# An audio-tower kernel: TensorE's attention product ahead of the transposes of the next pair's probabilities

## The reference

```python
h = tok(x)                         # importance of each row by a 2-layer GELU MLP, then pooling to 375 rows
h = h + attn(layernorm(h))         # 8 heads of 64, causal, with distance bias, q/k/v by a 3-tap filter
h = h + ffn(layernorm(h))          # 16 experts, each takes its top tokens; and one shared MLP
```

```python
q = split_heads(proj(xp, wq1, wqd)) * scale
k = split_heads(proj(xp, wk1, wkd))
v = split_heads(proj(xp, wv1, wvd))
sim = einsum("bhid,bhjd->bhij", q, k) + bias * slopes      # then masked to j <= i
out = einsum("bhij,bhjd->bhid", softmax(sim), v)
return out.transpose(0, 2, 1, 3).reshape(b, n, 512) @ wout.T
```

## Time and profile before

| | |
|---|---|
| median of 3 runs | 1357.37 us (1357.0 to 1360.63) |
| the profiled execution | 1359.58 us, its span 1357.8 us |
| TensorE busy (matmul) | 1199.7 us, 88% of the span, 7812 matmuls |
| TensorE weight loads | 1002.9 us, 74% |
| VectorE / ScalarE / GpSimd busy | 892.8 us (66%) / 731.9 us (54%) / 407.8 us (30%) |
| DMA | 42.94 MB, mean 32 GB/s |

### The profile page before, as it was taken

How to read it: one execution, slowest core, us unless ns; L and a number is a source line. 1 busy time by engine, 2 the same in 40 slices (tenths; PEclk the granted TensorE clock), 3 DMA queues, 4 the chain that set the end, 5 groups by cost and what they waited for, 6 DMA issues and landing times. The chain is left out here.

```text
span 1357.8 us, 23184 instructions
## 1 busy us (share of the span) xinstructions
PE 1199.7 (88%) x7812; PEld 1002.9 (74%) x7812; DVE 892.8 (66%) x2614; ACT 731.9 (54%) x1845; POOL 407.8 (30%) x379
## 2 busy tenths in 40 slices
PE   7999999999958999999999999999984998767663
PEld 6999999999946777777777777777763777555452
DVE  5656566665558888888888888988864878122210
ACT  2444534434346778887777888877872441322210
POOL 5000001300023323234443333441111000688885
PEclk9999999999958999999999999999997998987877
DMA  5000000000000000000000000000002000454542
GB/s 140 28 13 24 12 24 13 24 12 13 1 24 12 1 25 25 25 25 19 13 21 25 25 25 25 19 14 9 14 14 61 24 23 4 110 89 82 93 76 36
DMA packets 91800, 42.94 MB, mean 32 GB/s; under 512 B 31066, under 2 KB 88007, under 8 KB 91687
## 3 DMA queue, kind: packets, MB, share of 16 engines
q1 hardware_dynamic: 67207, 33.49, 9.1%
q0 software_dynamic: 23808, 6.69, 3.8%
q10 hardware_dynamic: 672, 1.31, 0.3%
HBM read 28.22 MB, written 9.65 MB: 28 GB/s over the span
## 5 line engine op out<-in xcount | busy, mean ns | idle before, releaser
L485 PE MATMUL bank<-h1hl,W2hl 128*128 128x376 f32 x1536 | 278.9, 337 | 2.6 <-DVE h1hl L638 2.6
L485 PEld LDWEIGHTS bank<-h1hl,W2hl 128*128 128x128 f32 x1536 | 265.2, 190 | 7.2 <-issue 4.3
L1051 ACT ACTIVATE P<-P,nmax 125x375 f32<-125x375 f32 (+2 forms) x384 | 188.9, 501 | 3.6 <-DVE nmax L1182 3.6
L585 ACT ACTIVATE h<-bank,b2c 128x375 f32<-128x375 f32 x128 | 73.6, 575 | 211.2 <-PE bank L485 211.2
L226 POOL TENSOR_SCALAR cellmax<-grid,csb 125x375 f32<-125x375 f32 x96 | 124.2, 1304 | 207.3 <-DVE csb L219 140.8
L1182 DVE CUSTOM_DVE_ANT_0 P<-bank,nbias 125x375 f32<-125x375 f32 (+2 forms) x384 | 138.9, 410 | 6.0 <-PE bank L888 5.8
L1061 ACT COPY PT<-bank 128x500 f32<-128x500 f32 (+1 forms) x256 | 127.3, 550 | 5.3 <-PE bank L907 3.1
L888 PE MATMUL bank<-QK 64*125 64x375 f32 (+2 forms) x768 | 117.7, 411 | 2.4 <-DVE nmax L1182 2.4
L901 PE MATMUL bank<-ident,P 125*128 125x125 f32 x768 | 111.1, 271 | 5.1 <-ACT P L1051 4.5
L1069 ACT ACTIVATE tap<-bank,qkd 128x375 f32<-128x375 f32 x128 | 68.6, 570 | 82.6 <-PE bank L941 82.5
L1649 ACT ACTIVATE hE<-bank,EB 128x375 f32<-128x375 f32 x64 | 36.7, 574 | 134.3 <-PE bank L1598 131.6
(11 more groups left out here) (209 smaller groups left out, 2304.1 us busy)
## 6 DMA issues: line engine op xcount, KB each, us to landing
X<-in_x_dram SPq DMA_DIRECT2D x31, 375.0 KB
EW<-in_L_ffn_w_dram SPq DMA_DIRECT2D x32, 256.0 KB
token_table<-row SPq DMA_DIRECT2D x16, 210.9 KB
tTall<-tT SPq DMA_DIRECT2D x16, 187.5 KB, 2.5
out_dram<-oS SPq DMA_DIRECT2D x16, 187.5 KB
tTall<-in_L_tok_W_dram ACTq DMA_DIRECT2D x1, 1024.0 KB, 8.8
EB<-in_L_ffn_b_dram SPq DMA_DIRECT2D x16, 62.5 KB
tok<-token_table,ids POOLq DMA_INDIRECT x48
```

What stands on the lines that cost most here:

```text
L485: last = nc.tensor.matmul(bank[4 + m % 2][:, :NE], W2hl[:, a, k, m * 128:(m + 1) * 128], h1hl[:, p, b, k], start=(k == 0 and n == 0), stop ...
L1051: nc.scalar.activation(P[:, 2 * r + q, SEG[i]:SEG[i] + w], P[:, 2 * r + q, SEG[i]:SEG[i] + w], ACT.Exp, bias=nmax[:, 2 * r + q, i:i + 1], ...
```

## The change

In TensorE's body, the call of `attend` is moved ahead of the call of `transpose_probs`. It is made in even half-steps only, so the odd ones are as they were.

```diff
--- before.py
+++ after.py
@@ -990,12 +990,12 @@
                                 transpose_v(n, e)
                             if valid(m):
                                 project_v(m, d, m % 2)
+                        m, d = pair_before(b, c, 2)
+                        if part == 0 and valid(m):
+                            attend(m, d, u if c >= 2 else v_)
                         m, d = pair_before(b, c, 1)
                         if valid(m):
                             transpose_probs(m, d, part)
-                        m, d = pair_before(b, c, 2)
-                        if part == 0 and valid(m):
-                            attend(m, d, u if c >= 2 else v_)
                         if h == 1 and ahead(b + 2):
                             pool_tokens(b + 2)
                         if h == 1 and valid(b - 2):
```

## The result

The changed kernel takes 1338.36 us, the median of 4 runs (1337.6 to 1338.85); the kernel before took 1358.7 us beside it (4 runs, 1357.0 to 1360.63). The ratio is 0.9849, with an interval of 0.9832 to 0.9866: faster by 1.5%. The prediction was 1337.7 us.

What follows compares the result with a forecast made beforehand. TensorE was taken as bound in some quarters of a body, a chain through ScalarE or VectorE in others. Bodies 10.7, start 1.9 and end 7.1 us made 19.7, taking the 1357.37 us median to 1337.7 (range 1327 to 1350).

Steps and rivals of the forecast that it cites:

- The exchange at nothing: TensorE's new neighbours, projection then product then transposes: costed at nothing, with 0.1 us a pair either way.
- Third pair: Half-step h = 4 of a body: the wait for precw goes and VectorE's tap comes earlier, 0.24 us gained.
- Fourth pair: Half-step h = 6: waits hide behind the product, VectorE no longer waits for ScalarE's tap, 0.42 us gained.
- First pair: Half-step h = 0: TensorE already follows VectorE's QK, so only 0.08 us, for ScalarE's earlier taps.
- Second pair: Half-step h = 2: of 0.47 us lost to precw, 0.10 comes back, as QK limits TensorE's start.
- Sum: The four pairs' gains together: 0.84 us a body, 10.7 us over the stage's 12 or 13 bodies.
- The start: First body's third pair: the product fills TensorE's 2.44 us wait, 1.9 us gained (bounds 1.3 and 2.4).
- the end: Last half-steps and the seven pairs before them: TensorE's waits filled, 7.1 us gained (bounds 4 and 8).
- VectorE as the bound throughout: Rival, chance 0.14: third and fourth pair give nothing, only start and end's 9.0 us stand, 1348.4 us.
- TensorE throughout: Rival, chance 0.10: TensorE is the bound everywhere, all losses come back, 1.64 us a body, 1327.6 us.
- Late copies: Rival, chance 0.06: later transposes make ScalarE hold the third and fourth pair, 17 us slower, 1375 us.
- No change: Rival, chance 0.08: the product runs earlier, but a wait of equal size follows everywhere, start and end too.

Runs made afterwards that it cites:

- e5: The changed kernel with an extra VectorE memset ahead of its taps for VT in the third and fourth pair: 1340.49 us, ratio 0.9858.
- e6: The kernel before the change, with an extra VectorE memset ahead of its taps for VT in the third and fourth pair: 1359.83 us, ratio 1.0007.
- e12: The changed kernel with V projected before V's transposes, and the third pair's low-part subtraction moved from VectorE to GpSimd: 1329.30 us, ratio 0.9776.
- e8: The changed kernel, but with the product left behind the transposes in the first pair of every body: 1340.04 us, ratio 0.9862.
- e1: The kernel before, with the product moved first in the third and fourth pair only: 1342.13 us, ratio 0.9868.
- e2: The kernel before, with the product moved first in the first and second pair only: 1356.53 us, ratio 0.9974.
- e9: The changed kernel with VectorE's cell overlap of h = 4 put behind its VT of h = 5: 1350.33 us, ratio 0.9935.
- e7: The changed kernel with the third pair's transposes of the normalised tokens put ahead of those of the probabilities: 1341.04 us, ratio 0.9867.
- e10: The changed kernel with V projected before V's transposes, and VectorE's cell overlap of h = 4 behind VT of h = 5: 1334.85 us, ratio 0.9822.

## Why the prediction was right, point by point

*The product fills the waits.* Right. The waits for `precw` are gone, and the transposes start behind the product without idling. No delay of its own came with the new neighbours. Projection to product is 695.57 - 694.33 = 1.24 us, and projection to transposes had been 703.90 - 702.75 = 1.15 by this row of before:
```profile
702.75 1.31 PE L941 MATMUL bank<-xnThl,WQKT 128*128 128x378 f32 x6
```
That is 0.09 us more. Product to transposes is 1.42, the same as product to L286 before. Behind L907 the product had started after 0.25 us and L286 starts after 0.11, 0.14 less. The exchange at nothing held, within 0.05 us.

*Third pair: mechanism right, size off.* Forecast 0.24 us, bounds -0.1 and 0.30; measured 3.73 - 3.35 = 0.38, outside the bounds. The step that failed is what ScalarE gets back. Its wait at the copy was taken at 0.08 and is 0.19, which speaks for less. But the forecast took the time between its instructions at their durations, and an instruction that need not wait starts sooner than that. From L296 to the copy of V it is 0.55 us (699.43 to 699.98) where the earlier trace rows have 0.80; of these 0.25 the forecast counted 0.14. From the copy of V to the tap it is 0.36 (699.98 to 700.34) where it was 0.52, and there the forecast counted nothing, since the tap stood 0.04 behind the copy's end and looked unwaited for. It was TensorE's projection of V that it followed, which ended at 709.13, 0.04 us ahead of it, as the first of these rows of the kernel before (timeline, third pair) shows:
```profile
708.37 0.76 PE L948 MATMUL bank<-xnThl,WVT 128*128 128x378 f32 x3
...
709.40 0.08 DVE L1182 DVE_READ_ACCUMULATOR2_ANT nmax<- 125x1 f32 x1
```
ScalarE's own sum is 0.18 + 0.25 + 0.16 - 0.19 = 0.40 us, against 0.38 at `VT`. (By start times the wait before `xnT` and the new one at the copy are both worth 0.29 us, so that the sum is the same.) The bound of 0.30, "all that VectorE idles", failed for the same reason on VectorE, by the second row: before, the tap followed the read of the maxima by 709.78 - 709.40 = 0.38 us, of which 0.08 are that read's record and 0.30 idle; now the two start together, at 700.98. The whole 0.38 came back.

*Fourth pair.* Forecast 0.42, bounds 0 and 0.66; measured 0.50, the 0.42 of idle time and again 0.08 of the read ahead of the tap. That VectorE had slack there and has none now is shown by e5 and e6; that it is the only bound is not (e12 finds ScalarE level with it).

*First pair.* Forecast 0.08, bounds 0 and 0.15; its own move is worth 0.03 (e8). The interval has 0.10 less, but the late pairs' moves bring it (e1).

*Second pair.* Forecast 0.10; measured 0.13 for the first and second pair together (e2), which with 0.03 for the first leaves 0.10. QK was what TensorE could not start before, and its wait for it, 0.26 us, stands in the waits.

*Sum.* Forecast 0.84 a body, measured 1.10. The third and fourth pair were forecast at 0.24 + 0.42 = 0.66 and gave 0.88. These are the terms that were mis-sized, and they make most of the 0.26, which is 3.1 us over twelve bodies. The start gave 2.67 against 2.4, the end 6.83 against 7.2. The start's 1.9 was right in size, but the forecast had no clock in it, and most of the gain in that pair is the clock's. The changed kernel's profiled execution had its third pooling 0.96 us later and a rest 0.58 longer, which hid a part: 21.2 us against 19.7. So it is in part luck that the median came within 0.7 us of the forecast; the mechanism was right, the sum of a body a quarter too small.

*VectorE as the bound throughout* (0.14) fell: by it the third and fourth pair give nothing. The rule of the Trainium skill behind it (Perfetto Trace Analysis, Identifying the Most-Contended Engine), weight loads' busy share for TensorE, puts TensorE at 29.12 us of 39.35 and VectorE at 33.89. This case's runs don't bear it out for what the change could gain: those two pairs gave 0.97 us. It is borne out in part one step later: with those waits gone VectorE has no slack there (e5), though ScalarE is level with it (e9, e12).

*TensorE throughout* (0.10) fell too: all its losses were 1.64 us a body, and 1.10 came back. *Late copies* (0.06): ScalarE waits 0.19 us, far below the 0.8 from which it decides; e7 shows its price, 0.31 us for 0.32 of waiting. *No change* (0.08) is excluded by the waits, which are gone with nothing of equal size in their place.

*What should have shown* in the profile mostly did: no waits for `precw`, short ones for QK, no wait for the tap in the fourth pair, a body of 38.5 us or below, and the projection of the third pair still waiting for VectorE (0.27 us, 0.36 before; the forecast had "as now or longer", and it is a little shorter). Two things differ. The waits for the exponential are not gone but are 27 short ones of the weight loads, with no idle time of the matmuls; and TensorE's wait for the maxima, 0.19 us in each third pair, was not forecast.

## What to carry to other kernels

Where an engine's in-order stream waits for another engine just ahead of work that needs nothing of that wait, put that work first; what it gives is not the wait's length but how far the next engine in the chain was itself late, read quarter by quarter of the loop from the wait that ends last. To tell whether an engine has slack in a place, add a small known load on it there, once in each version, and take the length of a loop body from the trace rather than the total time. To tell whether it is the only bound, take work away there as well: when engines are level, as here at 37.9 us a body, the load's whole delay is paid and the relief gives nothing. And look at what runs beside the work that an edit moves, since that changes too.

## What the runs showed of the hardware

- An instruction that doesn't have to wait starts before the recorded end of the one ahead of it: on ScalarE 0.36 us behind the start of a copy of 0.48, and 0.55 behind that of an activation of 0.67. With a wait for TensorE in them the same steps took 0.52 and 0.80, of which the durations leave 0.04 and 0.14 to see. On VectorE a tap that needs no wait starts together with the read of the maxima ahead of it, whose record is 0.08 us long. A row's idle time, or its lack, thus understates what a wait costs.
- A memset of 0.27 us on VectorE cost about 0.15 us a piece (0.29 us a body for two).
- VectorE's copy of 125 x 384 floats for `precw` takes 0.36 us in most pairs and 0.70 in the second pair of every kernel, where GpSimd's L276 and L279 run beside it, and in the fourth pair of e9 and e10, where L226 does. Beside GpSimd's L1135 and L1138, in the third pair, it stays at 0.36. No run tests why.
- In the first body the granted clock before was 0.76 from 428 to 432 us. It fell at 430, behind TensorE's wait of 2.44 us (to 428.88), to 0.50, which is 1.2 GHz; the product that began just ahead took 1.89 us, and the scores 1.62. In the changed kernel, with waits of 0.87 and 0.93 us there, the clock from 424 to 432 is 1.00 and the product takes 1.49. The fall had cost about 1.5 us of that pair.
- In kernels that are the same up to there the program's first pooling starts between 233.06 and 235.88 us. Why is open.
